# 500 row transfers of a graph kernel, issued over 128 partitions instead of 125

## What is computed

```
x = layernorm(x + segment_sum(message(x[src], x[dst], edge_attr, W1, W2), dst))
e = leaky_relu(s_src[src] + s_dst[dst])        # s_* = x @ attn_w halves
out = layernorm(x + segment_sum(softmax_by_dst(e) * x[src], dst))
```

## Time and profile before

| | us |
|---|---|
| Median of three runs | 6929.51 (6928.4 to 6939.59) |
| Time of the profiled execution | 6937.29 |
| Span of the profiled execution | 6935.5 |
| POOL busy | 4829.8 |
| DVE busy | 3611.6 |
| PE busy | 3336.5 |

### The profile page before, as it was taken

The page is one execution under the profiler, slowest core; times in us unless marked ns, Lnnn a source line. Parts: engine busy times, 40 slices in busy tenths (PEclk is TensorE's granted clock), DMA queues, the critical chain, the costliest instruction groups (busy, mean ns, idle before and its releaser), DMA issues. The chain is left out here.

```text
span 6935.5 us, 56399 instructions
## 1 busy us (share of the span) xinstructions
PE 3336.5 (48%) x12859; PEld 1619.6 (23%) x12859; DVE 3611.6 (52%) x5473; ACT 2498.8 (36%) x3555; POOL 4829.8 (70%) x4416
## 2 busy tenths in 40 slices
PE   0005999999999999999999980000000000000000
PEld 0003444444444444444444430000000000000000
DVE  4225888788887888888888862012222222212221
ACT  0005666666666666666666650000000000000000
POOL 4576777777777777777777628777666676677657
PEclk9999999999999999999999995555555555555555
DMA  3411111111111111111111101111111111111111
GB/s 138 160 39 36 30 28 30 30 29 30 30 30 30 30 28 27 31 31 29 30 31 30 23 13 11 12 21 25 26 27 21 29 25 24 24 25 25 24 26 20
DMA packets 275726, 228.08 MB, mean 33 GB/s; under 512 B 194512, under 2 KB 251465, under 8 KB 273006
## 3 DMA queue, kind: packets, MB, share of 16 engines
q0 software_dynamic: 131424, 79.08, 8.3%
q1 hardware_dynamic: 144082, 147.06, 6.6%
HBM read 137.03 MB, written 88.30 MB: 32 GB/s over the span
## 5 line engine op out<-in xcount | busy, mean ns | idle before, releaser
L1152 POOL DMA_INDIRECT gxb<-tab_d,idxb x1600 | 1537.3, 961 | 707.6 <-issue 626.2
L535 POOL DMA_INDIRECT gx<-in_x,idx x1540 | 1679.0, 1090 | 411.1 <-issue 368.4
L862 DVE TENSOR_TENSOR prod<-G_ps,hid 128x1000 f32<-128x1000 f32 x1200 | 1420.8, 1193 | 618.6 <-PE G_ps L738 303.9
L752 PE MATMUL R_ps<-sums,red 128*48 128x500 f32 x2400 | 1297.2, 624 | 0.0
L1244 PE MATMUL R_ps<-dm,ones 125*125 125x125 f32 x2 | 0.8, 494 | 2598.0 <-DVE dm L1273 2598.0
L631 ACT ACTIVATE FT<-T_ps 128x500 fp32r<-128x500 f32 x1200 | 707.0, 589 | 524.5 <-PE T_ps L721 323.0
L721 PE MATMUL T_ps<-ident,HL 125*128 125x125 f32 x4800 | 753.5, 280 | 270.1 <-ACT HL L625 189.5
L542 POOL TENSOR_TENSOR sums<-prod 128x500 f32<-128x500 f32 x400 | 502.7, 1257 | 516.3 <-DVE prod L862 312.4
L1159 ACT ACTIVATE ex<-ex 125x80 f32<-125x80 f32 x40 | 10.8, 269 | 2214.8 <-issue 1117.7
L1205 DVE TENSOR_TENSOR_SCAN Zb<-dec,Zb,wx 125x40 f32<-125x40 f32 x1280 | 333.3, 294 | 722.3 <-issue 721.3
L721 PEld LDWEIGHTS T_ps<-ident,HL 125*128 125x128 f32 x4800 | 574.1, 143 | 484.8 <-ACT HL L625 189.8
(11 more groups left out here) (190 smaller groups left out, 4268.7 us busy)
## 6 DMA issues: line engine op xcount, KB each, us to landing
y_d<-Zb SPq DMA_DIRECT2D x40, 664.1 KB
gx<-in_x,idx POOLq DMA_INDIRECT x1600
gxb<-tab_d,idxb POOLq DMA_INDIRECT x1600
xd_d<-zeros SPq DMA_DIRECT2D x16, 1562.5 KB
xv<-xd_d SPq DMA_DIRECT2D x40, 625.0 KB
y_d<-zr SPq DMA_DIRECT2D x40, 625.0 KB
em<-in_edge_attr SPq DMA_DIRECT2D x40, 195.3 KB
kp<-keep_d SPq DMA_DIRECT2D x40, 156.2 KB
```

Source lines behind the costliest of these rows:

```text
L535: nc.gpsimd.indirect_dma_start(out=gx[h][:, c * DIM:(c + 1) * DIM], out_offset=None, in_=x, in_offset=bass.IndirectOffsetOnAxis(idx[h][:, ...
L752: last = Tn.matmul(R_ps[0:NOUT, 0:GW], red[:, i * NOUT:(i + 1) * NOUT], sums2[k][:, i * GW:(i + 1) * GW], start=(i == 0), stop=(i == 2))
L862: V.tensor_tensor(prod[i][:, :].rearrange("p (a e) -> p a e", a=2), gv, hid[k][:, :].rearrange("p (a e) -> p a e", a=2), ALU.mult).then_in ...
L1152: nc.gpsimd.indirect_dma_start(out=gx[h][:, c * T1:(c + 1) * T1], out_offset=None, in_=tab_d, in_offset=bass.IndirectOffsetOnAxis(idx[h][: ...
```

## The change

The tiles that the five loops of 100 transfers read or write (`blk_i`, `blkbuf`, `first_i`, `last_i`, `xn`, `ng` in blocks c and e, `sd`) get 128 partitions instead of 125. The loops themselves take whole tiles, so their 500 transfers now have 128 rows each. Everything else still works on the first 125 partitions. The three spare partitions get harmless contents: index 0 in `blk_i` and `last_i`, an index of 2E in `first_i`, which the bounds check drops, zeros in `xn` and `sd`. For this POOL has three new memsets, DVE has two (`xn`, 128x3200, at the start, and `sd`, 128x100, in block c), SP waits for the memset of `xn` before it loads it, and DVE waits for POOL's three.

```
-        xn = sb("xn", [P, NP * DIM])
+        xn = sb("xn", [PG, NP * DIM])
-        first_i = sb("first_i", [P, NP], i32)
-        last_i = sb("last_i", [P, NP], i32)
+        first_i = sb("first_i", [PG, NP], i32)
+        last_i = sb("last_i", [PG, NP], i32)
-            blk_i = sbt("blk_i", [P, NP], i32)
+            blk_i = sbt("blk_i", [PG, NP], i32)
-            blkbuf = sbt("blkbuf", [P, NF * SB])
+            blkbuf = sbt("blkbuf", [PG, NF * SB])
...
-                    sp.dma_start(xn[:, :], x.rearrange("(p k) f -> p (k f)", k=NP)).then_inc(S("a_x"), 16)
+                    sp.wait_ge(S("a_xn0"), 1)
+                    sp.dma_start(xn[0:P, :], x.rearrange("(p k) f -> p (k f)", k=NP)).then_inc(S("a_x"), 16)
...
+                    nc.gpsimd.memset(blk_i[:, :], 0).then_inc(S("a_rowz"), 1)
+                    nc.gpsimd.memset(last_i[:, :], 0).then_inc(S("a_rowz"), 1)
+                    nc.gpsimd.memset(first_i[:, :], 2 * E).then_inc(S("a_rowz"), 1)
...
                     V.memset(zeros[:, :], 0.0).then_inc(S("a_zero"), 1)
+                    V.memset(xn[:, :], 0.0).then_inc(S("a_xn0"), 1)
+                    dve.wait_ge(S("a_rowz"), 3)
                     dve.wait_ge(S("a_dst"), 16)
...
-            ng = sbt("ng", [P, NP * DIM])
+            ng = sbt("ng", [PG, NP * DIM])
...
-            sd = sbt("sd", [P, NP])
+            sd = sbt("sd", [PG, NP])
...
+                    step(V.memset(sd[:, :], 0.0))
                     dve.wait_ge(S("c_carry"), 1)
...
-            ng = sbt("ng1", [P, NP * R1])
+            ng = sbt("ng1", [PG, NP * R1])
```

More of the change, by code:

```diff
@@ L319, in _ @@
                     step(V.tensor_scalar(tn[:, 0:NP], cnt[:, :], -1.0, 0.0, ALU.add, ALU.max))
-                    V.tensor_copy(blk_i[:, :], tn[:, 0:NP]).then_inc(S("a_blk"), 1)
+                    V.tensor_copy(blk_i[0:P, :], tn[:, 0:NP]).then_inc(S("a_blk"), 1)
                     for k in range(NP):
@@ L324, in _ @@
                             dve.wait_ge(S("a_fine"), k - NF + 1)
-                        V.tensor_scalar(junk[:, (k % NF) * JW:(k % NF) * JW + SB], blkbuf[:, (k % NF) * SB:(k % NF + 1) * SB], nodef[:, k:k + 1], None,
+                        V.tensor_scalar(junk[:, (k % NF) * JW:(k % NF) * JW + SB], blkbuf[0:P, (k % NF) * SB:(k % NF + 1) * SB], nodef[:, k:k + 1], None,
                                         ALU.is_le, ALU.add, accum_out=fine[:, k:k + 1]).then_inc(S("a_fine"), 1)
@@ L331, in _ @@
                     step(V.tensor_tensor(empty[:, :], endf[:, :], startf[:, :], ALU.is_equal))
-                    V.scalar_tensor_tensor(first_i[:, :], empty[:, :], float(E), startf[:, :], ALU.mult, ALU.add).then_inc(S("a_idx"), 1)
+                    V.scalar_tensor_tensor(first_i[0:P, :], empty[:, :], float(E), startf[:, :], ALU.mult, ALU.add).then_inc(S("a_idx"), 1)
                     step(V.tensor_scalar(tn[:, 0:NP], endf[:, :], -1.0, float(ZROW + 1), ALU.mult, ALU.add))
                     step(V.tensor_tensor(tn[:, NP:2 * NP], tn[:, 0:NP], empty[:, :], ALU.mult))
-                    step(V.scalar_tensor_tensor(last_i[:, :], endf[:, :], -1.0, tn[:, NP:2 * NP], ALU.add, ALU.add))
+                    step(V.scalar_tensor_tensor(last_i[0:P, :], endf[:, :], -1.0, tn[:, NP:2 * NP], ALU.add, ALU.add))
                     dve.wait_ge(S("a_w"), 32)
@@ L984, in piece_of @@
         def piece_of(ap, i, width):
-            return ap[:, i * KP * width:(i + 1) * KP * width].rearrange("p (k f) -> p k f", f=width)
+            return ap[0:P, i * KP * width:(i + 1) * KP * width].rearrange("p (k f) -> p k f", f=width)
         def layer_norm(dve, step, i, v, out_v, sq_t, st, key):
@@ L1064, in _ @@
                         step(V.tensor_tensor(sq, x1, bc(attn_b[:, DIM:2 * DIM]), ALU.mult))
-                        V.tensor_reduce(sd[:, i * KP:(i + 1) * KP], sq, AX.X, ALU.add).then_inc(S("c_sd"), 1)
+                        V.tensor_reduce(sd[0:P, i * KP:(i + 1) * KP], sq, AX.X, ALU.add).then_inc(S("c_sd"), 1)
                         dve.wait_ge(S("c_sd"), i + 1)
@@ L1078, in _ @@
                     sp.wait_ge(S("c_sd"), NPIECE)
-                    sp.dma_start(sdt_d.rearrange("(p k) a -> p (k a)", k=NP), sd[:, :]).then_inc(S("c_sdt"), 16)
+                    sp.dma_start(sdt_d.rearrange("(p k) a -> p (k a)", k=NP), sd[0:P, :]).then_inc(S("c_sdt"), 16)
                     sp.wait_ge(S("c_x1e"), NPIECE)
@@ L1317, in _ @@
                         part = slice(i * KP * DIM, (i + 1) * KP * DIM)
-                        sp.dma_start(out.rearrange("(p k) f -> p (k f)", k=NP)[:, part], xn[:, part]).then_inc(S("e_out"), 16)
+                        sp.dma_start(out.rearrange("(p k) f -> p (k f)", k=NP)[:, part], xn[0:P, part]).then_inc(S("e_out"), 16)
                     sp.wait_ge(S("e_out"), 16 * NPIECE)
```

## The result

After: median 6809.39 us (6803.31 to 6815.21, four runs); before, on the same chip, 6933.91 us (6928.4 to 6939.59, four runs). The ratio is 0.9822 (0.9807 to 0.9838), or 124.5 us less, with the interval some 112 to 134. The forecast was 6796, with a range of 6776 to 6832.

The account below looks back on a forecast made before the run. POOL's issuing of transfers was taken to bound the four plain loops, and the DMA engines partly the block fetches. Savings of 99 + 35 = 134 us from the 6929.5 us median gave 6796 us, range 6776 to 6832.

Parts of the forecast that it names:

- What bounds the loops: Two scatter loops and two loops fetching sums last as long as POOL needs to issue their 100 transfers each.
- Term 1: Two scatter loops and two loops fetching sums: 128-row transfers start every 1.25 us, saving 99 us together.
- Term 2: Block fetches: fewer packets per engine, so 2.1 us each beside the zero stores instead of 5.0; 35 us saved.
- Edits at nothing: New memsets by DVE and POOL are covered by other waits, and three spare rows add no time.
- Block b: The block with nearly all matmuls must keep its 3575 us; over 10 us different would make the prediction wrong.
- The first: Rival, chance 0.11: block fetches keep their pace while the zero stores run; 109 us saved, 6820 us.
- The second: Rival, chance 0.05: scatters keep 1.49 us at 128 rows, only fetches become cheaper; 85.5 us saved, 6844 us.
- The third: Rival, chance 0.03: three dropped rows of each feature and attention scatter are dear; about 46 us slower, 6976 us.
- The fourth: Rival, chance 0.02: a transfer's price hangs on something other than its rows, so only noise is left, 6929 us.

Follow-up runs that it names:

- blk_only: The kernel before with only the 100 block fetches at 128 rows, the other 400 transfers at 125; 6897.41 us, ratio 0.9958.
- half_stores: The changed kernel with its 16 zero stores cut into 32 of half the width; 6791.23 us, one run.
- wide_before: The kernel before, on the second chip, with its 16 zero stores over 128 partitions and no gates; 6603.84 us, ratio 0.9864.
- no_drop: The changed kernel, on a third chip, with a longer table so that no attention scatter row is dropped, bounds check only on the last fifty; 6813.78 us.
- row_counts: The changed kernel with the four pieces of block e fetched at 126, 127, 112 and 120 rows; 6861.72 us.

## Why the prediction was right

**What bounds the loops.** Right: POOL's issue time alone sets the four plain loops; their lengths fell with it, and DVE kept up.

**Term 1, 99 us.** Measured 96 (24.8 + 21.2 + 23.5 + 26.6). The sum is closer to 99 than its parts are, which is partly luck. By loop: a fetch did fall by 0.255 us (25.2 us in 99 distances). In block e the long calls shrank too (what they take over the median is 4.9 us in before, 3.2 in after), and in block c they grew from 6.2 to 10.1; they come in groups a piece apart, where DVE works on a piece, which I haven't tested. A scatter fell by only 0.206 us and not 0.245, as POOL works 0.98 us on one of 128 rows and not 0.95; that takes 7.7 us off the two loops. In its place came 8.5 us that I hadn't seen in my own trace: two extra pauses of 2.1 us in each scatter loop, which the smaller slot count removes. The group's idle column held them all the time, 34.7 us in the earlier trace rows where 99 steps of 0.30 give 29.7.

**Term 2, 35 us.** Measured 35.5 (33.5 in the window, 2.0 after it, as a fetch lands sooner). The mechanism held, but its pace and its end of the stores were both off: the pace under the stores was 2.37 us on average from 150 to 195 us, between my 2.1 (three turns) and 2.6 (four), but the stores ended earlier than the 306 that I had worked out (SP's queue is at 21.2% from 280 to 290 us, at 4.8% from 290 to 300 and empty behind), so the fetches had less of it to bear. That the window closed at 324.0 against 323 predicted is two errors that cancelled. Blk_only showed the term alone, and half_stores showed that it is turns and not bytes.

**Edits at nothing.** Right: the first block fetch starts at 133.6 us, as before. Not everything that follows the loops was free, though: the closing drain of POOL grew by 7.1 us in block a and by 6.4 in block c. The blocks behind start 6.6 and 6.2 us later for it. No part of the prediction has these 12.8 us, and they are the step that failed: the way from a loop to the next block was taken as unchanged, without a price for POOL's own close of the block. The median lies 13.4 us over the forecast. Of that, 4.4 come from a base of 6933.9 instead of 6929.5. The other 9 are the drains' 12.8 and the 3 that term 1 fell short, less small gains elsewhere (3.4 us, most of it in block d) and less some 3 us that the medians can't resolve.

**Block b.** Its window and the correction were 11.8 us shorter in after's profile, with the matmul count as before and POOL's and ACT's within a few us. It isn't the change: in the same measure the three traces with 125-row sums and scatters give 3621.6 us (before), 3626.1 (blk_only) and 3603.2 (wide_before), and the eight traces with 128 rows 3609.8 (after) to 3623.6 (no_drop), so the two groups overlap. The runs of either kernel spread over 11 or 12 us by themselves. The traces' difference of 134.0 us fits the predicted 134 only by this chance; the medians' 124.5 is the number to believe. I said that a block b off by over 10 us would make the prediction wrong; as a test of the change that was set too tight.

**Rivals.** The first (the pace kept) is refuted by blk_only and half_stores. The second (scatters stay at 1.49) by 1.29. The third (dropped rows dear) by no_drop, directly, and already by the 0.98 us of a scatter in after. The fourth by row_counts: the price changes with the number of rows alone, within one loop.

**Open.** What POOL does in the pauses and in the drain: the runs show a count that rises by slots and is cleared near 1020, and a drain that goes by scatters pending, nothing more. The 127-row fetches fit the same limit: they pause after seven of 128 slots each (896), and an eighth would make 1024, between the 1018 that went without a pause and the 1027 that didn't. But the 125-row fetches, with the same slots as the scatters, show no pause, although their closing drain in block e is as short as if there had been one, and the 126-row fetches ahead of those of 127 rows seem not to count. Open too is why DVE's counts and POOL's block d have no gaps on the second chip, and what varies in block b.

## What to carry to other kernels

Issue indirect transfers, and large stores too, over a row count with a large divisor up to sixteen: best 128, with harmless indices on the spare rows. For an indirect transfer it is worth some 0.2 to 0.25 us of POOL each, for a store the difference between five DMA engines and sixteen; check the number of packets in the trace first. When a small transfer shares its engines with a large one, count its packets per engine and the time that one of the other's packets takes: their product, plus the small transfer's own work, came near its pace in all three cases here (5.0, 2.4 and 1.4 us). And when a loop's price is read from two neighbouring lines, compare the group's idle time with count times step, and look at what the engine does between its last instruction and the next block.

## What was unexpected of the hardware

- The end of block a costs POOL 9 us after a hundred 128-row scatters: DRAIN 8.964 us, against 1.859 when a pause had cleared the first 78 and 0.140 when it had cleared 99. The pause that clears 99 takes 2.8 us, so one pause late in the loop is cheaper than leaving all to the drain.
- Among indirect fetches of 136-byte rows (block e) one row more or less changes the price from 0.98 us (126) to 2.55 (127) and to 0.95 (128).
- Stores of 1.6 MB from 125 partitions ran at 130 GB/s, from 128 partitions at some 390, with the first gathers running beside them.
- A fetch beside those stores went from 5.0 us (nine packets with data on an engine) to 2.4 (three) and to 1.4 (three, the store's packets half as large), with the same bytes to move.
